# Second linear attention with tokens on partitions, a column of ones in the values, and elu on ScalarE

## The reference, cut to the stage

```python
# x is (625, 768) after the first layer; xn is its layer norm
qkv = (xn @ w_qkv).reshape(B, N, 3, H, D)          # H = 12 heads, D = 64
q = jax.nn.elu(q) + 1.0
k = jax.nn.elu(k) + 1.0
attn = jnp.einsum('bhnd,bhmd->bhnm', q, k)
attn = attn / jnp.sum(attn, axis=-1, keepdims=True)
out = jnp.einsum('bhnm,bhmd->bhnd', attn, v)
out = out @ w_proj + b_proj                         # added to x
```

## Time and profile before

| | us |
|---|---|
| median of 3 runs | 2146.84 (2140.87 to 2151.06) |
| the profiled execution | 2146.55 |
| its span in the trace | 2144.5 |
| TensorE busy | 1901.9 (89%) |
| VectorE busy | 1348.9 (63%) |
| ScalarE busy | 904.6 (42%) |
| mean granted TensorE clock | 0.94 |
| first key matmul of the stage | 681.04 |
| first matmul of the next stage | 881.89 |

### The profile page before, as it was taken

One profiled execution on the slowest core, in us unless ns is written; L12 is line 12 of the kernel. 1 busy time (PEld: TensorE's weight loads), 2 busy tenths in 40 slices (PEclk: granted clock), 3 DMA queues, 4 the chain that ended last, 5 costly groups with the idle time before them and its releaser, 6 DMA issues.

```text
span 2144.5 us, 30883 instructions
## 1 busy us (share of the span) xinstructions
PE 1901.9 (89%) x12258; PEld 1806.1 (84%) x12259; DVE 1348.9 (63%) x2448; ACT 904.6 (42%) x1469; POOL 221.8 (10%) x169
## 2 busy tenths in 40 slices
PE   5978989979997985678876799999999999999998
PEld 4866879978887985567876789999999999999998
DVE  6997766343235566587777466335665656766787
ACT  2331114313131431276544422333555656666776
POOL 0000000012000000375541000000010100000110
PEclk9998998987999998789987999999999999999999
DMA  2110020100111110201002212225465656776896
GB/s 108 45 45 1 23 89 30 52 24 23 45 67 58 68 38 30 76 21 36 16 1 104 91 67 85 79 71 199 177 224 180 231 210 220 242 251 231 280 316 219
DMA packets 36795, 234.29 MB, mean 109 GB/s; under 512 B 5916, under 2 KB 7318, under 8 KB 14632
## 3 DMA queue, kind: packets, MB, share of 16 engines
q1 hardware_dynamic: 31318, 217.41, 28.4%
q0 software_dynamic: 2656, 8.99, 1.9%
q10 hardware_dynamic: 2674, 5.87, 0.7%
HBM read 221.91 MB, written 10.35 MB: 108 GB/s over the span
## 4 chain that ended last, share of the span: by engine, by line
PE 71%; DVE 15%; issue 8%; ACT 3%; DMA 2%; POOL 1%; SPq 0%; DVEq 0%; ACTq 0%; POOLq 0%
PE bank L312 15%; PE bank L314 14%; PE bank L313 14%; PE bank L2417 7%; PE bank L569 3%; PE bank L2418 3%; PE bank L2429 3%; DVE weight_lo L285 2%; PE bank L2433 2%; PE bank L2421 1%; PE bank L2430 1%; PE bank L2432 1%; DVE mix_kv L792 1%; PE bank L2420 1%; POOL gat_edge L1793 1%
## 5 line engine op out<-in xcount | busy, mean ns | idle before, releaser
L285 DVE TENSOR_TENSOR weight_lo<-weight_raw,weight_hi 128x2304 fp32r<-128x2304 f32 (+1 forms) x155 | 389.1, 2513 | 41.6 <-ACT weight_hi L275 41.4
L275 ACT ACTIVATE weight_hi<-weight_raw 128x2304 fp32r<-128x2304 f32 (+1 forms) x155 | 323.1, 2087 | 89.2 <-DMA weight_raw<-in_ffn_w 48.7
L312 PE MATMUL bank<-xT_hi,weight_hi 128*128 128x306 f32 (+1 forms) x576 | 184.3, 320 | 6.4 <-DVE mix_kv L1576 2.5
L313 PE MATMUL bank<-xT_lo,weight_hi 128*128 128x306 f32 (+1 forms) x576 | 178.9, 311 | 0.0
L314 PE MATMUL bank<-xT_hi,weight_lo 128*128 128x306 f32 (+1 forms) x576 | 178.6, 310 | 0.0
L312 PE MATMUL bank<-weight_hi,xT_hi 128*128 128x384 f32 (+1 forms) x480 | 161.5, 336 | 9.8 <-DVE xT_lo L333 4.5
L2791 DVE TENSOR_TENSOR hidden_tmp<-hidden_tmp,bank 128x160 f32<-128x160 f32 (+5 forms) x192 | 65.6, 341 | 158.6 <-ACT hidden_tmp L2577 158.6
L313 PE MATMUL bank<-weight_lo,xT_hi 128*128 128x384 f32 (+1 forms) x480 | 157.6, 328 | 0.0
L314 PE MATMUL bank<-weight_hi,xT_lo 128*128 128x384 f32 (+1 forms) x480 | 157.5, 328 | 0.0
L569 PE MATMUL bank<-one_hot_dst,one_hot_src 125*128 125x313 f16 x800 | 122.6, 305 | 15.2 <-ACT packed_counts L583 7.9
L312 PE MATMUL bank<-weight_hi,hidden_hi 128*128 128x384 f32 (+1 forms) x366 | 124.4, 340 | 0.0
(11 more groups left out here) (477 smaller groups left out, 5254.4 us busy)
## 6 DMA issues: line engine op xcount, KB each, us to landing
weight_raw<-in_ffn_w SPq DMA_DIRECT2D x111, 1152.0 KB, 5.2
weight_raw_fifth<-in_ffn_w SPq DMA_DIRECT2D x25, 1152.0 KB, 5.2
weight_raw<-in_shared_w SPq DMA_DIRECT2D x16, 1152.0 KB, 5.3
weight_raw<-in_mix_kv SPq DMA_DIRECT2D x8, 1152.0 KB, 6.2
weight_raw<-in_gat_w SPq DMA_DIRECT2D x8, 768.0 KB, 4.3
weight_raw<-in_mix_q SPq DMA_DIRECT2D x4, 1152.0 KB, 5.2
weight_raw<-in_mix_out SPq DMA_DIRECT2D x4, 1152.0 KB, 5.1
weight_raw<-in_gnn_w SPq DMA_DIRECT2D x4, 1152.0 KB, 5.1
```

The costliest lines, as they stand in the source:

```text
L275: act.activation(upper_, whole_, ACT.Copy).then_inc(*w_hi.one())
L285: dve.tensor_tensor(lower_, whole_, upper_.bitcast(F32), ALU.subtract).then_inc(*w_lo.one())
L312: pe.matmul(dst, a[0], b[0], start=first, stop=False)
L313: pe.matmul(dst, a[0], b[1], start=False, stop=False)
```

## The change

The stage is rewritten and its neighbours follow.

- The chunk order becomes keys, values, queries of pairs 0 to 2, then keys, values, queries of pairs 3 to 5, then the two output chunks.
- Elu: ScalarE takes Relu(-x) from the bank, then Exp(-that), which is exp(min(x, 0)); VectorE adds max(x, 0) from the bank; then the upper and lower halves, piece by piece, in three work buffers. The copy to SBUF and the minimum on VectorE are gone. Values are halved straight from the bank.
- Each head's 64 value columns have a 65th of ones, so `per_head` yields the sums of the keys as a column; the ten matmuls with ones per pair are gone. Head halves are made from the bank, ScalarE and VectorE, two small blocks per pair.
- All queries are kept (`qp` for six pairs). `attend` works per token tile: the queries are stationary, the pair's 130 columns move, three pairs to a bank, six heads' denominators are six columns. The reciprocal has six elements per token.
- The attended tile is turned by six transposes on TensorE, halved, and projected with both output chunks at once (18 matmuls a bank), two banks a tile. A tile's projection alternates with the attention of the tile two ahead and the turning of the next.
- Both output chunks are now freed at the end of the stage, and the split of the chunk that waits for the first moves into the next stage's `prepare` (after its fifth tile).
- The two bias rows are loaded together, added to each other and then to x, on VectorE after the first keys.

```diff
-    order += mix_order("mix1")
+    order += ([("mix1_kv", 0), ("mix1_kv", 1), ("mix1_q", 0), ("mix1_kv", 2), ("mix1_kv", 3), ("mix1_q", 1)]
+              + [("mix1_out", i) for i in range(2)])
...
         def tensor():
...
             def per_head(grp):
-                pk, pv = (2 * grp) % KV, (2 * grp + 1) % KV
-                pe.wait_ge(*kv_lo.at(2 * grp + 2))
+                pe.wait_ge(*elu_lo.at(KEYS[grp] + TT))
+                pe.wait_ge(*kv_lo.at(TT * (grp + 1)))
                 for pr in range(3):
...
+                    product(bank[:, 0:PW], [(at(kp, slice(0, n), t, slice(pr * P, (pr + 1) * P)),
+                                             at(vp, slice(0, n), t, slice(2 * pr, 2 * pr + 2), ALL))
+                                            for t, n in enumerate(SIZES)]).then_inc(*heads_full.one())
+
+            def attend(t):
+                n = ROWS[t]
+                pe.wait_ge(*elu_lo.at(MADE))
+                for g in range(2):
+                    pe.wait_ge(*att_lo.at(6 * (g + 1)))
+                    bank = ring.next(o_ready.at(2 * t + g + 1))
+                    o_banks.append(bank)
+                    for pr in range(3):
+                        end = product(bank[0:n, pr * PW:(pr + 1) * PW],
+                                      [(at(qp, ALL, 3 * g + pr, slice(t * P, t * P + n)), at(att, ALL, 3 * g + pr, ALL))])
+                    end.then_inc(*o_full.one())
+
+            def turn(t):
...
+                    for k in range(3):
+                        end = pe.transpose(bank[:, k * P:k * P + n], outs[0:n, t % 2, (3 * g + k) * P:(3 * g + k + 1) * P], ident[0:n, 0:n])
+                    end.then_inc(*o_turned.one())
+
+            def project(t, c):
...
+                product(bank[0:n, 0:HALF], [(at(outT, ALL, t % 2, 3 * i + k, slice(0, n)), at(w[i], ALL, k, slice(c * HALF, (c + 1) * HALF)))
+                                            for i in range(2) for k in range(3)]).then_inc(*out_full.one())
+
+            keys(0)
+            values(0)
+            queries(0)
             per_head(0)
...
+            keys(1)
+            values(1)
+            queries(1)
             per_head(1)
...
+            attend(0)
+            attend(1)
+            turn(0)
+            for t in range(TT):
+                if t + 2 < TT:
+                    attend(t + 2)
+                project(t, 0)
+                if t + 1 < TT:
+                    turn(t + 1)
+                project(t, 1)
...
         def scalar():
...
+            def elu(j, bank, wide, dst, dst_free=None):
+                part = work[:, j % WORK, 0:wide]
+                if j >= WORK:
+                    act.wait_ge(*elu_lo.at(j - WORK + 1))
+                act.activation(part, bank, ACT.Relu, scale=-1.0).then_inc(*elu_low.one())
+                act.wait_ge(*elu_low.now())
+                act.activation(part, part, ACT.Exp, scale=-1.0).then_inc(*elu_exp.one())
+                act.wait_ge(*elu_made.at(j + 1))
+                if dst_free:
+                    act.wait_ge(*dst_free)
+                upper(dst, part).then_inc(*elu_hi.one())
...
+            per_head(1)
+            weight_read[c0 + 5] = q_full.at(12)
+            turned(0)
+            weights_hi(c0 + 5)
+            turned(1)
+            turned(2)
+            weight_read[c0 + 6] = weight_read[c0 + 7] = out_full.at(2 * TT)
+            weights_hi(c0 + 6)
+            turned(3)
+            turned(4)
...
         def vector():
+            def elu(j, bank, wide, dst):
+                part = work[:, j % WORK, 0:wide]
+                dve.wait_ge(*elu_exp.at(j + 1))
+                dve.scalar_tensor_tensor(part, bank, 0.0, part, ALU.max, ALU.add).then_inc(*elu_made.one())
+                dve.wait_ge(*elu_made.now())
+                dve.wait_ge(*elu_hi.at(j + 1))
+                lower(dst, part).then_inc(*elu_lo.one())
...
+            def attend(t):
...
+                    own_step(dve.reciprocal(inverse[0:n, g, :], by_head[:, :, DH]))
+                    dve.wait_ge(*(o_turned.at(2 * (t - 2) + g + 1) if t >= 2 else row_added.at(1)))
+                    dve.tensor_tensor(outs[0:n, t % 2, g * HALF:(g + 1) * HALF].rearrange("p (h d) -> p h d", d=DH), by_head[:, :, 0:DH],
+                                      inverse[0:n, g, :].unsqueeze(2).broadcast_to([n, HG, DH]), ALU.mult).then_inc(*o_ready.one())
...
+            keys(0)
+            weights_lo(c0)
+            biases()
+            values(0)
+            weights_lo(c0 + 1)
+            queries(0)
             per_head(0)
...
@@ -1922,6 +1942,8 @@
                     if step == TT - 1:
+                        if grp == 0:
+                            weights_hi(c0 - 1)
                         weight_read[w1_chunk(grp)] = h_full.at(TT * (grp + 1))
...
@@ -2041,6 +2063,8 @@
                     dve.wait_ge(*scored.now())
+                    if step == TT - 1 and grp == 0:
+                        weights_lo(c0 - 1)
                     if step == TT - 1 and grp < 3:
                         weights_lo(w1_chunk(grp))
```

More of the change, by code:

```diff
@@ new lines, in queries @@
+            def queries(grp):
+                w = weight("mix1_q", grp)
+                for n in range(3):
+                    for s, (a0, wide) in enumerate(SPANS):
+                        bank = ring.next(elu_made.at(QUERIES[grp] + 2 * n + s + 1))
+                        q_banks.append(bank)
+                        product(bank[:, 0:wide], [(at(w, ALL, k, slice(n * P, (n + 1) * P)), at(xT, ALL, k, slice(a0, a0 + wide)))
+                                                  for k in range(KD)]).then_inc(*q_full.one())
@@ L1387, in per_head @@
                     head_banks.append(bank)
[L1388 to L1409, removed]
-                    o_banks.append(bank)
-                    product(bank[:, 0:wide], [(at(att, ALL, n, ALL), q)]).then_inc(*o_full.one())
-                    bank = ring.next(o_ready.at(2 * (2 * n + s) + 1))
-                    o_banks.append(bank)
-                    product(bank[:, 0:wide], [(at(den, ALL, n, ALL), q)]).then_inc(*o_full.one())
@@ new lines, in turned @@
+            def turned(t):
+                n = ROWS[t]
+                act.wait_ge(*heads_full.at(6))
+                if t >= 2:
+                    act.wait_ge(*out_full.at(2 * (t - 2) + 2))
+                for g in range(2):
+                    act.wait_ge(*o_turned.at(2 * t + g + 1))
+                    upper(at(outT, ALL, t % 2, slice(3 * g, 3 * g + 3), slice(0, n)),
+                          turn_banks[2 * t + g][:, 0:3 * P].rearrange("p (k n) -> p k n", n=P)[:, :, 0:n]).then_inc(*o_hi.one())
@@ new lines, in scalar @@
+            act.wait_ge(*pads_blank.at(1))
+            for half in att:
+                act.activation(half[:, :, :], blank, ACT.Copy).then_inc(*pads_hi.one())
+            act.activation(vp[0][:, :, :, DH], ones_f[:, 0:TT * HG].rearrange("p (t h) -> p t h", t=TT), ACT.Copy).then_inc(*pads_hi.one())
+            act.activation(vp[1][:, :, :, DH], work[:, 0, 0:TT * HG].rearrange("p (t h) -> p t h", t=TT), ACT.Copy).then_inc(*pads_hi.one())
+            act.wait_ge(*pads_hi.now())
+            keys(0)
@@ L1603, in vector @@
+            dve.memset(work[:, :, :], 0.0).then_inc(*pads_blank.one())
+            dve.wait_ge(*pads_hi.at(4))
+            keys(0)
+            weights_lo(c0)
+            biases()
+            values(0)
+            weights_lo(c0 + 1)
+            queries(0)
+            per_head(0)
+            weights_lo(c0 + 2)
+            keys(1)
+            weights_lo(c0 + 3)
+            values(1)
+            weights_lo(c0 + 4)
             queries(1)
             per_head(1)
-            dve.wait_ge(*att_hi.at(1))
@@ L1619, in vector @@
+            attend(1)
+            turned(0)
+            weights_lo(c0 + 5)
+            for t in range(TT):
+                if t + 2 < TT:
+                    attend(t + 2)
+                project(t, 0)
+                if t + 1 < TT:
+                    turned(t + 1)
+                if t == 2:
                     weights_lo(c0 + 6)
[L1620 to L1622 removed]
+                project(t, 1)
         tensor()
```

333 lines of the change are left out of this document (123 added, 210 removed).

## The result

The changed kernel takes 2094.86 us (median of 4 runs, 2091.71 to 2098.23) where the kernel before takes 2147.31 (4 runs, 2140.87 to 2151.06): ratio 0.9759, 95% interval 0.973 to 0.9788. Measured again, among other kernels, it took 2098.15 (5 runs), ratio 0.9774, 0.975 to 0.9797. The prediction was 2100, with a range of 2092 to 2112. The profiled execution after took 2091.71 us, span 2089.8.

The account below looks back on a forecast made before the run. The prediction took TensorE's chain as the bound, with 48.9 of the stage's 200.85 us waiting and half clock. From 2146.55 it took 51.2 gained in the stage and added 4.8 given back in the next: 2100.2, range 2092 to 2112.

Follow-up runs that it names:

- e2: The kernel after without look-ahead, each token tile attended, turned and projected before the next: stage 164.59 us against 147.95, total 2107.88 us.
- e3: The kernel after with an unread 384-column reciprocal added ahead of each of the ten short ones: stage 161.27 us against 147.95, total 2102.64 us.
- e9: The kernel after with attention one tile ahead of the projections instead of two: stage 148.83 us against 147.95, total 2093.21 us.
- e10: The kernel after with the moved weight split ahead of the dots and the store of x issued behind the fifth product h: total 2092.24 us.
- e7: The kernel after with the moved split ahead of the next stage's dots and its neighbour's split behind has_edge: dots 14.26 us against 16.34, total 2091.48 us.

## What to carry to other kernels

In this kernel a microsecond of TensorE's waiting had two prices, its own and mostly the lower clock behind it (e2: 9.4 us of waits, 16.6 us of time; e3: 8.0 and 13.3; e9 with one wait of 0.6 us kept 1.00); so count TensorE's work at full clock first, and take the rest as the prize. One tile of other work between a product and its consumer was nearly all the cover that was needed, and a second one under 1 us. When a transfer is moved ahead of one that is on the path, look at which of the transfers in flight is the large one without a waiter: here the store took over 4 us of delay and the rows some 0.4. Look too at what stands next in the same queue: the hidden bias landed 2 us later, and once the rows were early (e10) the first dot hung on it.

## What the hardware showed that was not expected

Some operations of VectorE and GpSimd don't run side by side. VectorE and GpSimd of after:

```profile
856.20 2.03 DVE L2086 CUSTOM_DVE_ANT_0 gat_edge<-gat_edge,edge_terms 128x640 f32<-128x640 f32 x1 [1.91 <-POOL edge_terms L1800]
858.16 0.81 DVE L2086 CUSTOM_DVE_ANT_0 gat_edge<-gat_edge,edge_terms 128x640 f32<-128x640 f32 x1
...
862.88 1.39 DVE L2145 TENSOR_TENSOR gat_total<-gat_total,gat_has_edge 128x2 f32<-128x2 f32 x1
...
862.71 1.54 POOL L1800 TENSOR_TENSOR edge_terms<-gat_edge_log,gat_src_row 128x640 f32<-128x640 f32 x1 [0.84 <-DVE gat_minus_peak L2086]
```

The same operation takes 2.03 us when GpSimd's second edge term is still running (a pair from 854.53 that lasts 3.02 us) and 0.81 behind it. A product of two columns takes 1.39 us and ends at 864.27, where GpSimd's operation, begun at 862.71, ends at 864.25. It works the other way too: e7's split of 1.75 us on VectorE made GpSimd's pair 1.3 us longer. The Trainium skill, "SBUF — State Buffer", section "SBUF: two separate sides", describes the two engines' common port pair as an exclusive lock held for a whole instruction when a VectorE operation has two inputs in SBUF and the GpSimd operation reads SBUF; these rows agree with it. So e7's split took its usual 1.75 us on VectorE and cost GpSimd 1.3 us besides.
